# A Perceiver layer on one core: the shared expert's MLP moved into the span attention, chunk by chunk

## What is computed

```python
x = x + cross_attention(layernorm(x), ctx, ctx)       # 16 heads, 1601 keys a batch
x = x + span_attention(layernorm(x))                  # 16 heads, keys weighted by distance from a learned mean
x = x + ffn(layernorm(x))

# ffn, with tokens numbered 0..2047
shared = (silu(xf @ sw1 + sb1) * (xf @ sw3 + sb3)) @ sw2 + sb2        # 256 -> 512 -> 256
for k in range(2):                                    # routed by a hash of the token's number
    e = (tok * 11 + k * 7919) % 8
    out += gelu(xf @ w1[e] + b1[e]) @ w2[e] + b2[e]   # 256 -> 256 -> 256
ffn = (shared + out / 2) / 2
```

## Time and profile before

| | |
|---|---|
| median of 3 runs | 1594.85 us (1592.32 to 1598.48) |
| the profiled execution | 1592.08 us |
| its span, first to last instruction | 1590.3 us |
| mean granted TensorE clock | 0.979 of full |
| busy: TensorE / weight loads / VectorE / ScalarE / GpSimd | 1504.2 / 1265.2 / 1015.3 / 941.3 / 424.5 us |
| second part | from about 1299 us to the end |

### The profile page before, as it was taken

One profiled execution on the slowest core, in us unless ns is written; L12 is line 12 of the kernel. 1 busy time (PEld: TensorE's weight loads), 2 busy tenths in 40 slices (PEclk: granted clock), 3 DMA queues, 4 the chain that ended last, 5 costly groups with the idle time before them and its releaser, 6 DMA issues. The chain is left out here.

```text
span 1590.3 us, 56667 instructions
## 1 busy us (share of the span) xinstructions
PE 1504.2 (95%) x23708; PEld 1265.2 (80%) x23708; DVE 1015.3 (64%) x4006; ACT 941.3 (59%) x1836; POOL 424.5 (27%) x549
## 2 busy tenths in 40 slices
...
GB/s 154 142 112 109 108 109 109 108 109 123 128 116 109 113 116 116 113 115 111 118 109 123 112 106 111 109 108 108 109 108 108 67 96 74 2 1 8 61 21 54
DMA packets 89855, 156.26 MB, mean 98 GB/s; under 512 B 44784, under 2 KB 53744, under 8 KB 89328
## 3 DMA queue, kind: packets, MB, share of 16 engines
...
q0 software_dynamic: 288, 1.05, 0.2%
...
## 5 line engine op out<-in xcount | busy, mean ns | idle before, releaser
L666 DVE CUSTOM_DVE_ANT_0 junk<-bank,mask_q 128x400 bf16<-128x400 f32 (+1 forms) x1024 | 554.8, 571 | 196.1 <-issue 194.9
L618 ACT ACTIVATE probs<-bank 128x512 f32<-128x512 f32 (+1 forms) x832 | 469.4, 597 | 229.6 <-PE bank L792 188.6
L594 POOL CAST ctx_hi<-ctx_raw 128x400 fp32r<-128x400 f32 x248 | 122.1, 521 | 850.2 <-PE bank L756 850.2
L792 PE MATMUL bank<-qstack,kstack 104*128 104x128 f16 (+1 forms) x3328 | 306.1, 220 | 7.0 <-ACT probs L618 3.7
L773 PE MATMUL bank<-kstack,qstack 96*128 96x400 f16 (+1 forms) x1024 | 306.1, 338 | 3.6 <-DVE part_max L666 2.6
L792 PEld LDWEIGHTS bank<-qstack,kstack 104*128 104x128 f16 (+1 forms) x3328 | 220.2, 99 | 81.0 <-issue 26.3
L756 PE MATMUL bank<-wv_hi,ctx_hi 128*128 128x256 f32 (+1 forms) x832 | 279.9, 336 | 0.0
L597 POOL TENSOR_TENSOR ctx_lo<-ctx_raw,ctx_hi 128x400 fp32r<-128x400 f32 x248 | 253.3, 1043 | 0.0
L638 ACT ACTIVATE v<-bank 128x256 f32<-128x256 f32 (+1 forms) x416 | 159.7, 384 | 149.5 <-PE bank L756 137.1
L657 DVE SCALAR_TENSOR_TENSOR k_lo<-bank,bk,k_hi 128x400 f16<-128x400 f32 (+1 forms) x256 | 157.0, 632 | 128.2 <-ACT k_hi L628 128.1
L756 PE MATMUL bank<-wv_lo,ctx_hi 128*128 128x256 f32 (+1 forms) x832 | 233.2, 280 | 0.0
...
## 6 DMA issues: line engine op xcount, KB each, us to landing
...
kstack<-k_hi SPq DMA_DIRECT2D x512, 100.1 KB, 2.2
kstack<-k_lo SPq DMA_DIRECT2D x256, 100.1 KB, 2.2
weight<-in_w SPq DMA_DIRECT2D x18, 256.0 KB, 2.7
...
out_yT<-x SPq DMA_DIRECT2D x1, 2048.0 KB, 6.4
...
```

Source lines behind the costliest of these rows:

```text
L594: nc.gpsimd.tensor_copy(c_hi[:, k, s0:s0 + n], raw[:, k, s0:s0 + n]).then_inc(ctx_hi, 1)
L618: nc.scalar.activation(probs[kt % NP][0:m, GROUPS * h:GROUPS * (h + 1), :], st[h][0:m, :], ACT.Exp, scale=DK ** -0.5 / (UP * UP)).then_inc ...
L666: nc.vector.tensor_tensor_reduce(junk[i % SM][:, 0:n], sm[i % SM][:, 0:n], w["mask_q"][:, s0:s0 + n], 1.0, -3.0e38, ALU.add, ALU.max, part ...
L792: mm = nc.tensor.matmul(st[h][0:m, g * PW:(g + 1) * PW], kstack[b.slot][0:KROWS, p, kt * P:kt * P + m], qstack[b.slot][0:KROWS, p, :], sta ...
```

## The change

`tail`, `span_attention` and `expert_mlps` become one function with one order per engine for the whole second part. What differs in it:

- **Tokens** are split once per chunk, right after n (steps H on ScalarE, h on VectorE), from xc[1], in place of h2, into `tokens` [128, 2, 8 classes, 256], both parts for all tokens.
- **The shared expert** runs per chunk of 512 tokens. F (4 a chunk, one for each 128 of the 512 hidden features): 6 matmuls with sw1 to proj[0], 6 with sw3 to proj[1], 512 columns each; ScalarE F silu, VectorE F gate product, ScalarE G hi part, VectorE G lo part. G on TensorE (1 a chunk): 24 matmuls of 512 columns to proj[0] and proj[1]. VectorE r adds it to x.
- **The experts** per class: K on TensorE (24 matmuls of 256 columns; banks 4, 5 or 6, 7 in turn), K gelu and P hi on ScalarE per expert, P lo on VectorE, P on TensorE (24 matmuls to an ln bank). VectorE K is x plus bias into `y` (3 buffers), Y the result into y.
- **Stores** per class, 256 KB, into an output whose columns are sorted by class; the host's transposition changes with it.
- **Weights**: the pieces are sw1, sw3, sw2 first; all w1 and w2, alternating, after the last tokens are split. SP issues two loads, then a store, for each class.
- `ex` lies in attn_out's memory, o2 in rs.

The three orders:

```diff
-    PE_ORDER = """W0 M0 W1 V0 W2 S0 W3 T0 A0 M1 A0 A0 A0 A0 V1 A0 A0 S1 A0 T1 X0 U0 X0 M2 A1 X0 X0 V2 O0 S2 A1 Z0 A1 T2 A1 M3 m0 A1 A1
-        V3 A1 v0 A1 X1 X1 U1 X1 X1 A2 S3 O1 T3 A2 Z1 A2 A2 m1 A2 A2 A2 A2 v1 X2 X2 U2 X2 X2 A3 O2 A3 Z2 A3 A3 m2 A3 A3 A3 A3
-        v2 X3 X3 U3 X3 X3 O3 Z3 m3 v3"""
...
+    PE_ORDER = """W0 M0 W1 V0 W2 S0 W3 T0 A0 M1 A0 A0 A0 A0 V1 A0 A0 S1 A0 T1 X0 U0 X0 M2 A1 X0 X0 V2 O0 S2 A1 Z0 A1 T2 A1 m0 A1 M3 A1
+        v0 A1 V3 A1 X1 U1 X1 F0 A2 X1 X1 F0 S3 O1 F0 A2 Z1 A2 T3 A2 F0 m1 A2 A2 A2 v1 A2 G0 U2 F1 A3 X2 X2 F1 X2 X2 F1 O2 F1
+        A3 Z2 A3 G1 A3 m2 A3 A3 A3 A3 v2 X3 X3 U3 X3 X3 F2 O3 F2 Z3 F2 m3 F2 v3 G2 F3 K0 F3 K1 F3 K2 P0 F3 K3 P1 G3 K4 K5 P2
+        P3 P4 K6 P5 K7 P6 P7"""
+    DVE_ORDER = """W0 C0 W1 N0 W2 R0 W3 D0 C1 D0 D0 D0 D0 N1 D0 D0 R1 D0 b0 C2 D1 N2 O0 R2 D1 Z0 D1 D1 c0 D1 C3 D1 D1 n0 D1 h0 F0 N3 D2
+        G0 F0 G0 O1 R3 F0 D2 G0 Z1 D2 D2 c1 D2 F0 D2 G0 n1 D2 D2 h1 r0 F1 D3 G1 F1 G1 F1 O2 G1 F1 D3 G1 Z2 D3 r1 D3 c2 D3 D3
+        D3 D3 n2 h2 F2 O3 G2 F2 G2 Z3 F2 c3 G2 F2 G2 n3 h3 r2 F3 G3 P0 F3 G3 P0 F3 G3 P1 P1 P2 P2 F3 G3 P3 P3 r3 K0 Y0 K1 Y1
+        K2 K3 K4 Y2 P4 K5 P4 Y3 P5 K6 P5 Y4 K7 P6 Y5 P6 P7 Y6 P7 Y7"""
+    ACT_ORDER = """Q0 I0 S0 T0 B0 E0 B0 B0 Q1 E0 B0 E0 B0 E0 I1 E0 B0 B0 E0 E0 S1 B0 E0 T1 X0 L0 X0 U0 B1 Q2 X0 X0 I2 E1 S2 B1 B1 E1 T2
+        B1 E1 E1 B1 q0 E1 B1 Q3 E1 B1 i0 E1 B1 I3 E1 H0 X1 L1 X1 U1 F0 B2 X1 G0 X1 F0 G0 S3 E2 F0 B2 G0 E2 B2 T3 B2 E2 E2 F0
+        B2 B2 q1 E2 G0 E2 i1 B2 B2 H1 E2 E2 L2 U2 F1 B3 X2 G1 X2 F1 X2 G1 X2 F1 G1 E3 F1 B3 G1 E3 B3 E3 B3 E3 B3 B3 q2 E3 B3
+        E3 B3 E3 i2 E3 X3 H2 X3 L3 X3 U3 X3 F2 G2 F2 G2 F2 G2 q3 F2 G2 i3 H3 F3 G3 K0 P0 F3 K0 G3 P0 K1 F3 K1 G3 P1 K2 P1 K2
+        P2 P2 F3 G3 K3 K3 P3 P3 K4 K4 K5 K5 P4 P4 P5 P5 K6 K6 P6 P6 K7 P7 K7 P7"""
```

SP and GpSimd:

```diff
+    pieces = ["sw1", "sw3", "sw2"]
+    NFIRST = len(pieces)
+    pieces += [(w, i) for i in range(E + 1) for w in ("w1", "w2")]
...
+            def store(n):
+                sp.wait_ge(s["f_done"], NK * (n + 1))
+                dst = out_dram.rearrange("(k p) (e t) -> p k e t", p=P, e=E)[:, :, order[n], :]
+                sp.dma_start(dst, y[n % 3][:]).then_inc(y_out[n % 3], 16)
...
+            for n in range(NFIRST + 2 * (W_SLOTS + 1)):
+                load_weight(n)
+            for n in range(E):
+                for i in range(2):
+                    if NFIRST + 2 * (W_SLOTS + 1 + n) < len(pieces):
+                        load_weight(NFIRST + 2 * (W_SLOTS + 1 + n) + i)
+                store(n)
...
+                if n == NFIRST:
+
+                    pool.wait_ge(s["tok_lo_done"], NCH)
+                    pool.wait_ge(rstd_done[1], NCH)
+                    pool.wait_ge(s["x2_done"], NK * NCH)
```

VectorE and TensorE:

```diff
+            def add_shared(c, _):
+
+                for m in range(NK):
+                    dve.wait_ge(s["shared"], NK * c + m + 1)
+                    to = by_class(x[:, m, toks(c)])
+                    nc.vector.tensor_tensor(to, class_cols(proj[m][:, :]), to, ALU.add).then_inc(s["shared_done"], 1)
+
+            def biased_x(n, _):
+                if n == 0:
+                    dve.wait_ge(s["shared_done"], NK * NCH)
+                if n >= 3:
+
+                    dve.wait_ge(y_out[n % 3], 16 * (n // 3))
...
+            def proj_free(m):
+
+                need(pe, s["x1_done"], NK * emitted["W"])
+                need(pe, s["x2_done"], NK * emitted["Z"])
+                need(pe, s["silu_done"] if m == 0 else s["gate_done"], emitted["F"])
+                need(pe, s["shared_done"], NK * emitted["G"])
...
+            def shared_hidden(c, m):
+                pe.wait_ge(s["tok_lo_done"], c + 1)
+                pe.wait_ge(s["w_lo_done"], pieces.index("sw3") + 1)
+                for j, (weights, done) in enumerate(((sw1, s["f1"]), (sw3, s["f3"]))):
+                    proj_free(j)
+                    out = proj[j][:, :].rearrange("p (e t) -> p e t", e=E)
+                    accumulate(out, [(columns(weights, k, m), [chunk_tokens(part, k, c) for part in range(2)])
+                                     for k in range(NK)]).then_inc(done, 1)
+                emitted["F"] += 1
+
+            def shared_output(c, _):
+                pe.wait_ge(s["w_lo_done"], pieces.index("sw2") + 1)
+                pe.wait_ge(s["gate_lo_done"], FT * (c + 1))
+                for m in range(NK):
+                    proj_free(m)
+                    accumulate(proj[m][:, :], [(columns(sw2, k, m), [part[:, k, :] for part in gate_parts])
+                                               for k in range(FT)]).then_inc(s["shared"], 1)
+                emitted["G"] += 1
...
+                pe.wait_ge(s["w_lo_done"], split_count("w1", n))
+                for j, e in enumerate(CLASS_EXPERTS[order[n]]):
...
+                pe.wait_ge(s["w_lo_done"], split_count("w2", n))
+                pe.wait_ge(s["gelu_lo_done"], 2 * (n + 1))
```

More of the change, by code:

```diff
@@ L846, in cross_attention @@
     return {"sync": sync, "vector": vector, "gpsimd": gpsimd, "scalar": scalar, "tensor": tensor}
[L849 to L943, removed]
@@ L967, in span_attention @@
     BLOCKS = CW // P
[L968 to L976, removed]
@@ L977, in span_attention @@
-    b_copy = [sb(f"b_copy{i}", [P, CW]) for i in range(2)]
-    dist = [sb(f"dist{i}", [P, CW]) for i in range(2)]
-    ex = sb("ex", [P, PAIRS, CW])
-    vbd = sb("vbd", [P, CB, D])
-    rs, o2 = sb("rs", [P, NK, CW]), sb("o2", [P, NK, CW])
-    proj, ln_bank, ab, vb = bank[0:2], bank[2:4], bank[4:6], bank[6:8]
-    factors = [ab, vb]
-    names = ("x1_proj x1_done x2_proj x2_done span e0_done lnx_abs lnx_exp lnx_done vec packed_zero vbd_zero turn_ready packed_done turned "
-             "rows_done ab_ready b_copied dist_done ex_done sums lns_done rs_done val_ready vbd_done pv o2_done h_done").split()
@@ L1312, in expert_mlps @@
+    assert max(i for i, step in enumerate(PE_ORDER.split()) if step[0] == "W") < min(PE_ORDER.split().index(step) for step in ("Z0", "F0"))
     order, arrival = [0], list(CLASS_EXPERTS[0])
@@ L1316, in expert_mlps @@
         arrival.append(next(e for e in CLASS_EXPERTS[c] if e != arrival[-1]))
-    pieces = ["sw1", "sw3"] + [("w1", i) for i in range(W_SLOTS)]
+    pieces = ["sw1", "sw3", "sw2"]
     NFIRST = len(pieces)
-    pieces += ["sw2"] + [("w2", i) for i in range(W_SLOTS)] + [(w, i) for i in range(W_SLOTS, E + 1) for w in ("w1", "w2")]
-    def split_count(w, n):
-        return pieces.index((w, n + 1)) + 1
-    def slot_of(w, n, e):
-        return {"w1": w1, "w2": w2}[w][(n if arrival[n] == e else n + 1) % W_SLOTS]
@@ L1524, in expert_mlps @@
-    return {"sync": sync, "gpsimd": gpsimd, "scalar": scalar, "vector": vector, "tensor": tensor}
+    pieces += [(w, i) for i in range(E + 1) for w in ("w1", "w2")]
+    names = ("x1_proj x1_done x2_proj x2_done span e0_done lnx_abs lnx_exp lnx_done vec packed_zero vbd_zero turn_ready packed_done turned "
+             "rows_done ab_ready b_copied dist_done ex_done sums lns_done rs_done val_ready vbd_done pv o2_done h_done h2_done "
+             "tok_hi_done tok_lo_done f1 f3 silu_done gate_done gate_hi_done gate_lo_done shared shared_done fe gelu_done gelu_hi_done "
+             "gelu_lo_done xb_done f_out f_done w_halved w_hi_done w_lo_done w_in sel_in f_in").split()
```

860 lines of the change are left out of this document (459 added, 401 removed).

## The result

The changed kernel took 1598.65 us (median of 20 runs, 1596.63 to 1602.75), the kernel before 1591.95 us on the same chip (20 runs, 1584.54 to 1600.79): a ratio of 1.0049, with an interval of 1.0037 to 1.0061. It is slower: by 6.7 us in the medians, by 7.8 us by the ratio, whose interval lies wholly above 1. 1585 was forecast, 9.4 us faster than the 1594.85 that the first 3 runs had given. The profiled execution took 1597.29 us, with a span of 1595.5 us and a mean granted clock of 0.981.

What follows compares the result with a forecast made beforehand. Engines waiting in turn bound span attention, TensorE alone the stage behind it. 1377.35 + 165.7 work + 14 and 15.5 waits + 4 clock + 4.3 end = 1580.9 of span, 9.4 less than before: 1585 forecast, range 1567 to 1603.

Steps and rivals of the forecast that it cites:

- The place of the work: Span attention's last three chunks: 32.8 us of TensorE holes in 86.1 us, into which 50.6 us of F and G move.
- The work by pitch: TensorE matmuls priced by distance between starts: F step 2.81 us, G step 5.62, experts 45.0; width itself brings nothing.
- the ceiling of 165.7: All TensorE work from the first X1 on at full length without waits, 165.7 us against 206 before.
- Waits before the tokens: TensorE from the first X1 to the last chunk's tokens: single waits summing to 15.0 us, taken as 14.
- Not the bound on the mean: ScalarE up to the tokens: busy 82 of some 118 us, including 12 table loads at 1.28 us.
- Behind the tokens: TensorE after the last tokens: waits of 15.5 us, including 4.8 before K5 and 4.2 before P4.
- Clock: Granted clock: denser order removes most of the slow stretches, waits bring some back; 4 us added, ends 0 and 10.
- End: Last matmul to span's end: 4.3 us instead of 7.7, with the 256 KB store landing in 2.7.
- the store lands late: Rival: 256 KB stores take 6.4 us to land, delaying P4, P5, P6 and the end; 9 us lost, 1604; chance 0.20.
- Halved waits: Rival: the waits before and after the tokens are half of the 29.5 us counted; 15 us less, 1570; chance 0.18.
- Slow VectorE: Rival: VectorE slows while GpSimd splits weights behind the tokens; 4 us, 1589; chance 0.10.
- loads of ScalarE in the chain: Rival: ScalarE bounds the A runs, 8 of 12 table loads unhidden before E or B; 10 us, 1595; chance 0.04.

Runs made afterwards that it cites:

- shared behind: Kernel with one table set, weight loads ahead of stores and gelu_lo before biased x, but F, G, r of chunks 0 to 2 behind v3: 1.0078, 1603.41 us.
- one table: Changed kernel, with ScalarE naming the set holding both Exp and Ln again after each silu: ratio 0.9974 to the kernel before, 1585.28 us.

## Why the prediction was wrong, step by step

The measured 1598.65 lies in the range (1567 to 1603) and on the other side of no change.

1. **The place of the work, right.** For 50.6 us of fill the stretch up to the tokens was to grow from 86.1 to 117.9, so that 18.8 of the 32.8 us of holes would be used. With the surplus loads gone it measured 118.5, so 18.2; in the changed kernel 131.4, so 5.3. (The 28.7 us of shared behind are counted in that kernel's own stretch of 96.6 us, which has more holes.) The work by pitch was right too: with the surplus waits gone, the part behind the tokens takes 64.4 us against 61.8, and the whole stretch 177.9 against the ceiling of 165.7.
2. **Waits before the tokens: the step that failed.** It gave 14 us, of 117.9 in all; measured are 131.4, 13.5 more. The 12 table loads that the step counted and called "mostly hidden" were wrong twice. They were 23, since I took E, S and i for users of one set, where a load came at each change between Exp and Ln once a silu had intervened. And a surplus load was not hidden: taking 11 away moved the tokens by 12.9 us. "Not the bound on the mean" (82 of 118) did not bear on it: S, E and U stand on ScalarE in front of what TensorE and VectorE wait for, and there a load delays them whatever the share. With one table set there are exactly the 12 loads of the forecast and the stretch measured 118.5, beside 117.9. The sum's other terms for it hold as a total, then; whether those 12 loads are hidden, as it said, no run shows.
3. **Single waits.** Z1 was forecast at 1.8; it is 3.41, and 1.31 with one table. Z2 had 1.3 and measured 1.77, or 1.21. O3 (3.09) and U3 (2.26) stood at 1.9 for X3 and O3 together; with one table O3 has 0.51 and U3 less, so that these two are the loads again. Z3, G1 and F2 came as forecast (1.1, 1.2 and 1.7): 1.13, 1.22 and 1.69. My own sign of failure, gaps beyond 2 us before the tokens, is in the profile. That proj is shared was seen, that each Z waits for both banks at once was not: per-bank waits gave 6.4 us alone.
4. **Behind the tokens, nearly right.** Forecast 81.3 (61.8 work, 15.5 waits, 4 clock), measured 85.7. Both gaps are where they were put. K5: 4.8 forecast, 5.68 measured, of which 0.7 is the landing of 3.62 instead of 2.9. (The terms listed for it add up to 7.4, not the 7.6 written, so that 4.6 was its sum.) P4: 4.2 forecast, 6.20 measured: the working followed Y2 and the landing, but not SP's queue, on which store(2) stood 2.3 us behind a load; it then took 3.17 to land. K0's 2.5 and F3's 2.1 became 2.55 and 2.46, P7's 1.9 became 1.50. What is left, 85.7 - 61.8 - 18.4 = 5.5, stood at 4. It is the clock: three stretches with TensorE at work and the clock at 0.50, 11 us in all, of which half is 5.5. The forecast had two of them.
5. **Clock.** Above 0.90 up to the tokens, as said (0.96, then 1.00 twice). Behind them 0.89: the matmuls right behind K5's and P4's gaps start at 0.55 us instead of 0.36. It returns to 0.95 with both gaps removed and to 1.00 with K0's and K1's gone too. The stretches at half, behind K0's, K5's and P4's waits of 2.55, 5.68 and 6.20 us, columns as above:

```profile
1513.90:1517.20 3.30, 3.30 (x18) 3.30 (x17) 0.00 (x0) 1.46 (x3) 2.76 (x4) 0.50 0.41 122
1554.42:1558.10 3.68, 3.68 (x17) 3.68 (x18) 0.27 (x2) 0.73 (x2) 0.00 (x0) 0.50 0.28 71
1571.11:1575.10 3.99, 3.99 (x19) 3.99 (x20) 2.80 (x6) 0.00 (x0) 1.03 (x1) 0.50 0.35 121
```

6. **End.** 4.3 forecast, 3.4 measured. That the store lands late (0.20) was the rival for slower; it is refuted, 2.2 us.
7. **The rivals.** Halved waits (1570): no. Slow VectorE: `tokens_lo` lies before GpSimd's run now and takes 0.69, every time; gelu_lo has 1.79 at most beside a median of 0.69. Five of its 16 take 1.10 to 1.79, all five started while a GpSimd instruction ran and ended 0.54 to 0.56 us behind that one's end; the other eleven started while none ran and take 0.68 to 0.69. So the effect exists; it is 3.4 us of VectorE in all, and what of it reached TensorE was not tried. The right one had 0.04: loads of ScalarE in the chain, 10 us, 1595. That its 10 us come near the 12.9 is luck: it took 8 of the 12 counted loads, where the time lay in 11 loads that nobody had counted. The Trainium skill (ScalarE: Activation LUTs, What ACT_TABLE_LOAD costs) adds a drain of some 1.38 us to each switch; in the rows above the ACTIVATE starts 1.29 or 1.30 us after its load's start wherever both are shown, so no drain is seen here. The same page of the Trainium skill (Table sets: the hidden batching unit) says that Exp and Ln have a set in common, so that one load serves both; in the changed kernel that was not so behind a silu, and with that set named again it was.

The balance: forecast 9.4 less; 13.5 (tokens) + 4.4 (behind them) - 0.9 (end) = 17.0 more than forecast, so 7.6 us slower by the trace, beside 6.7 measured.

What took the gain is not one cost. By the ratios, the change without the fill (shared behind) stands 0.0078 above the kernel before; the fill brings 0.0204 (32 us); the surplus loads (12), the store in front of the loads (7.5) and the biased x between the gelu_lo (9) take 0.0175 (28 us) back, which leaves the 0.0049 measured (each step is the difference of two kernels that were run, so the sum must close). The two-bank wait is in both kernels with the fill and so not in this sum; without it the fill would bring 6 to 8 us more.
